# The last convolution layer of a four-layer image network: 1x1 products first, depthwise taps second, in place of convolutions folded into stacked planes

## The reference, cut to what matters

```python
def _edffn(x, w_in, w_dw, fft_w, w_out):          # x: group-normed, 48 channels
    h = jnp.einsum('bchw,oc->bohw', x, w_in)       # 1x1 products: 48 -> 192 channels
    h = conv(h, w_dw, 'SAME', feature_group_count=192)   # depthwise 3x3 taps
    x1, x2 = jnp.split(h, 2, axis=1)               # 96 and 96 channels
    h = gelu(x1, approximate=False) * x2
    y = jnp.einsum('bchw,oc->bohw', h, w_out)      # 96 -> 48 channels
    # 8x8 patches: f = rfft2(patch) * fft_w; y = irfft2(f)
    return y
x = x + _edffn(_gn(x), ...)
```

## Time and profile before

| | us |
|---|---|
| median of 3 runs | 21097.66 |
| the profiled execution | 21103.45 |
| its span, first to last instruction | 21101.9 |
| TensorE busy | 19033.5 (90%) |
| VectorE busy | 13401.1 (64%) |
| GpSimd busy | 10333.9 (49%) |
| ScalarE busy | 7503.4 (36%) |
| mean granted TensorE clock | 0.955 |

### The profile page before, as it was taken

How to read it: one execution, slowest core, us unless ns; L and a number is a source line. 1 busy time by engine, 2 the same in 40 slices (tenths; PEclk the granted TensorE clock), 3 DMA queues, 4 the chain that set the end, 5 groups by cost and what they waited for, 6 DMA issues and landing times. The chain is left out here.

```text
span 21101.9 us, 501412 instructions
## 1 busy us (share of the span) xinstructions
PE 19033.5 (90%) x172464; PEld 11794.6 (56%) x172464; DVE 13401.1 (64%) x22319; ACT 7503.4 (36%) x22720; POOL 10333.9 (49%) x8692
## 2 busy tenths in 40 slices
PE   6998998989989989899899898999998989898999
PEld 4665455456655554566555445665555456565666
DVE  4444445656667776666677766666777667777744
ACT  3554232145542221455422214663222122222222
POOL 0000000067767740677677406886774078787810
PEclk9999999999999999999999999999999999999999
DMA  3231112655533336455333364553434666666633
GB/s 92 68 70 45 35 36 84 140 112 113 113 99 111 110 119 145 109 112 113 99 110 111 112 151 111 121 121 100 111 110 126 134 146 150 149 149 146 147 88 78
DMA packets 932423, 2318.18 MB, mean 110 GB/s; under 512 B 276340, under 2 KB 528504, under 8 KB 844124
## 3 DMA queue, kind: packets, MB, share of 16 engines
q1 hardware_dynamic: 500560, 1364.68, 27.8%
q0 software_dynamic: 430080, 928.96, 16.7%
HBM read 1915.53 MB, written 385.13 MB: 109 GB/s over the span
## 5 line engine op out<-in xcount | busy, mean ns | idle before, releaser
L1840 POOL DMA_INDIRECT e_got<-table,e_idx x6144 | 7479.2, 1217 | 2580.1 <-issue 1603.5
L1856 POOL DMA_INDIRECT e_got<-table,e_idx x2048 | 2553.1, 1247 | 691.6 <-issue 501.7
L1010 PE MATMUL b_p_conv<-b_z,b_diag 32*32 32x512 f32 x76032 | 2807.1, 599 | 3.3 <-issue 3.3
L530 PE MATMUL a_p_qk<-a_wst,a_stack 125*128 125x192 f32 x12288 | 2466.8, 337 | 230.9 <-ACT a_qh L661 214.0
L530 PEld LDWEIGHTS a_p_qk<-a_wst,a_stack 125*128 125x128 f32 x12288 | 2025.8, 191 | 670.5 <-issue 367.5
L1112 ACT ACTIVATE b_z<-b_p_z 128x256 f32<-128x256 f32 x2112 | 846.5, 401 | 4026.9 <-PE b_p_z L974 3608.2
L1894 DVE TENSOR_TENSOR e_got<-e_got,e_wt 128x1536 f32<-128x1536 f32 x1024 | 1778.6, 1752 | 684.9 <-DMA e_got<-table,e_idx 682.3
L1199 DVE TENSOR_TENSOR b_ym<-b_p_in,b_mask 128x512 f32<-128x512 f32 x1056 | 729.4, 691 | 1807.8 <-PE b_p_in L966 1807.6
L974 PEld LDWEIGHTS b_p_z<-const,b_ym 128*128 128x128 f32 x8448 | 1165.3, 198 | 1215.5 <-issue 713.3
L974 PE MATMUL b_p_z<-const,b_ym 128*128 128x128 f32 x8448 | 1541.1, 307 | 100.1 <-ACT b_z L1112 93.9
L2140 PE MATMUL d_p_v<-d_xs,d_ws 125*128 125x512 f32 x4608 | 1388.2, 449 | 64.0 <-issue 60.4
(11 more groups left out here) (291 smaller groups left out, 35444.6 us busy)
## 6 DMA issues: line engine op xcount, KB each, us to landing
e_got<-table,e_idx POOLq DMA_INDIRECT x8192
b_x<-planes SPq DMA_DIRECT2D x264, 395.1 KB
a_stack<-in_xp SPq DMA_DIRECT2D x256, 387.0 KB
c_stack<-planes SPq DMA_DIRECT2D x256, 387.0 KB
d_stack<-planes SPq DMA_DIRECT2D x512, 193.5 KB
table<-i_acc SPq DMA_DIRECT2D x256, 384.0 KB, 2.3
b_xr<-planes SPq DMA_DIRECT2D x264, 197.5 KB
planes<-b_out SPq DMA_DIRECT2D x264, 197.5 KB
```

Source lines behind the costliest of these rows:

```text
L530: m = pe.matmul(dst_, st[:, row, dx + 128 * t:dx + 128 * t + 128], wst[:, dx, 0:2 * C2], start=(dx == 0), stop=False)
L1010: mm = pe.matmul(p_conv[q // 2 * 2 + r % 2][BLK * c:BLK * (c + 1), :], diag[g][BLK * r:BLK * (r + 1), k, :], zs[BLK * r:BLK * (r + 1), g, ...
L1840: pool.indirect_dma_start(out=self.got[q][:, t, c * REC:(c + 1) * REC], out_offset=None, in_=self.flat, in_offset=bass.IndirectOffsetOnAxi ...
L1856: pool.indirect_dma_start(out=self.got[q][:, t, c * REC:(c + 1) * REC], out_offset=None, in_=self.flat, in_offset=bass.IndirectOffsetOnAxi ...
```

## The change

`layer3` is written anew; the gathers, the spectrum, the residual and all other layers stay. `load_half` is gone.

- Loads: instead of 22 DMAs into stacked planes, a strip has 2: the same 49 planes of 9 rows go to partitions 0 to 48 and 64 to 112 of `x`.
- 1x1 products, in full fp32, into two PSUM banks `p_z`: for each of 4 quarters, two products of two rows each. `hidden_big` makes 128 channels by 64x128 tiles (2 in a pair), `hidden_small` the other 64 channels by 64x32 tiles (8), at two row offsets, so that a block of 32 channels lies twice on the partitions.
- ACT copies each quarter (128x1024) from `p_z` to `z` in SBUF, and once a strip two rows that the next strip needs.
- Depthwise taps as products with diagonal matrices: `taps_big`, 9 rounds (one for each tap) of sixteen 32x32 tiles into all four banks `p_v`; `taps_small`, 6 rounds of eight 64x32 tiles into two of them.
- ACT takes 3 gelus of 128x512 (before 6 of 64x512), DVE makes 3 products of 128x512 (before 6 of 64x512). `upper` and `lower` are gone from this layer.
- PSUM: `p_a` serves both the product with `w_out` and the spectrum (before `p_a` and `p_b`), one bank `p_c` the way back and the turned boxes (before two). A strip's taps need all four banks, so the next strip's taps wait for all products of this one.
- Beats: 64 in 3 strips as before, now counted over 15 rounds of taps a strip. DVE's order of box parts and products is new.
- Weights: 6 DMAs at the start of an image instead of 16, among them the image's first three rows.

```diff
+                def hidden_big(i, xs, row):
+                    r = 64 * i
+                    return pe.matmul(p_z[:, i, :], w[r:r + CP, 0:128], xs[r:r + CP, row:row + QROWS, 1:1 + W], start=True, stop=True)
+                def hidden_small(bank, r, xs, row):
+                    for t in range(4):
+                        y = row + t % 2
+                        mm = pe.matmul(p_z[BLK * t:BLK * t + BLK, bank, :], w[r:r + CP, 128 + BLK * t:128 + BLK * t + BLK],
+                                       xs[r:r + CP, y:y + QROWS, 1:1 + W], start=True, stop=True)
+                def hidden(n, xs, j):
+                    g, h = divmod(j, 2)
+                    pe.wait_ge(z_copied, n * 4 + j)
+                    for i in range(2):
+                        row = 2 * QROWS * h + QROWS * i
+                        mm = hidden_small(i, 64 * i, xs, row) if g else hidden_big(i, xs, row)
+                    mm.then_inc(h_ready, 1)
...
+                    def taps_big(lo, hi):
+                        if lo == 0:
+                            pe.wait_ge(z_copied, (n + 1) * 4)
+                            pe.wait_ge(zrow_ready, n + 1)
+                            pe.wait_ge(g_ready, n * 3)
+                        for i in range(lo, hi):
+                            dy, dx = divmod(i, 3)
+                            for row in range(4):
+                                for c in range(4):
+                                    q = PERM[row][c]
+                                    mm = pe.matmul(p_v[q // 2 * 2 + row % 2][BLK * c:BLK * (c + 1), :], diag[0][BLK * row:BLK * (row + 1), i, :],
+                                                   z[k][BLK * row:BLK * (row + 1), 0, dy:dy + SROWS, dx + QX * q:dx + QX * (q + 1)],
+                                                   start=(i == 0), stop=(i == 8))
+                    def taps_small(lo, hi):
+                        if lo == 0:
+                            pe.wait_ge(g_ready, n * 3 + 1)
+                        for i in range(lo, hi):
+                            y, dx = divmod(i, 3)
+                            for row in range(2):
+                                for c in range(4):
+                                    mm = pe.matmul(p_v[row][BLK * c:BLK * (c + 1), :], diag[1][64 * row:64 * (row + 1), i, :],
+                                                   z[k][64 * row:64 * (row + 1), 1, y:y + SROWS, dx + QX * c:dx + QX * (c + 1)],
+                                                   start=(i == 0), stop=(i == 5))
...
+                    # TensorE's order in a strip
+                    ahead(0); turn_box(0); taps_big(0, 3); w_out(0); turn_box(1); ahead(1); taps_big(3, 6)
+                    spectrum(0); ahead(2); taps_big(6, 9); inverse(0, 0); w_out(1); ahead(3)
+                    taps_small(0, 2); inverse(0, 1); spectrum(1); taps_small(2, 4); inverse(1, 0)
+                    taps_small(4, 6); inverse(1, 1)
...
+                    # VectorE's order in a strip
+                    box residual; box_part(0); [box residual]; box_part(1); scale(0); box_part(2)
+                    product(0); product(1); residual(0, 0); box_part(3); residual(0, 1)
+                    scale(1); residual(1, 0); product(2); residual(1, 1)
```

More of the change, by code:

```diff
@@ L2136, in conv_big @@
[L2136 to L2143, removed]
-                        mm = pe.matmul(out, we[i][0:NREST, lo:lo + 128], part(xe[j][0:NREST, :, :], side), start=False, stop=(i, j) == HALVES[-1])
-                    mm.then_inc(conv_ready, 1)
@@ L2147, in conv_small @@
-                def conv_small(bank, i, h, beats):
-                    tiles = [(bank[SMALL * k:SMALL * k + SMALL, :], HID * (k // 2) + BIG, k % 2) for k in range(4)]
-                    rows = slice(HROWS * h, HROWS * (h + 1))
-                    for dx in range(3):
-                        for out, lo, side in tiles:
-                            mm = pe.matmul(out, wst[:, dx, lo:lo + SMALL], part(stack[i][:, rows, dx:dx + W], side), start=(dx == 0), stop=False)
-                        if dx in beats:
-                            boxes.beat(mm)
-                    for k, (out, lo, side) in enumerate(tiles):
-                        mm = pe.matmul(out, wrs[0:NREST, lo:lo + SMALL], part(rest[i][0:NREST, rows, 0:W], side), start=False, stop=True)
-                        if k == 0 and 3 in beats:
-                            boxes.beat(mm)
-                    mm.then_inc(conv_ready, 1)
+                    pe.matmul(p_v[0][:, 0:NW], fold[:], win[:], start=True, stop=True).then_inc(folded, 1)
@@ L2162, in step @@
+                    pe.wait_ge(w_ready, 2 * (b + 1))
+                    hidden_big(0, x0, 0)
+                    hidden_small(1, 0, x0, 0).then_inc(folded, 1)
+                    pe.wait_ge(loaded0, (b * U + 1) * 32)
+                    pe.wait_ge(zrow_ready, n0 + 1)
+                    for j in range(4):
+                        hidden(n0, x[0], j)
                 def step(v, r, n, front, back, more):
                     m = n - 1
+                    k = r % 2
+                    units = turned(v, r) if boxes and back else []
@@ new lines, in ahead, with turn_box @@
+                    def ahead(j):
+                        if more:
+                            if j == 0:
+                                pe.wait_ge(loaded[1 - k], (b * U + v * 3 + (r + 1) // 2 + 1) * 32)
+                            hidden(n + 1, x[1 - k], j)
+                    def turn_box(j):
+                        if j < len(units):
+                            if j == 0:
+                                pe.wait_ge(res_ready, m * 4)
+                            else:
+                                boxes.bank_free(pe, *units[0])
+                            boxes.turn(pe, *units[j], p_c)
@@ L2203, in step @@
[L2203 to L2221 removed]
+                    ahead(0)
@@ new lines, in step @@
+                    turn_box(0)
+                    if front:
+                        taps_big(0, 3)
+                    if back:
+                        w_out(0)
+                    turn_box(1)
+                    ahead(1)
+                    if front:
+                        taps_big(3, 6)
+                    if back:
+                        spectrum(0)
+                    ahead(2)
+                    if front:
+                        taps_big(6, 9)
+                    if back:
+                        inverse(0, 0)
+                        w_out(1)
@@ L2338, in step @@
[L2338 to L2359 removed]
+                        dve.tensor_tensor(rows, p_c[0:CP, :].rearrange("p (t y x) -> p t y x", y=SROWS, x=16), rows, ALU.add).then_inc(res_ready, 1)
@@ new lines, in step @@
+                    if units:
+                        boxes.residual(dve, *units[0], p_c)
+                    box_part(0)
+                    if len(units) > 1:
+                        boxes.residual(dve, *units[1], p_c)
+                    box_part(1)
+                    if back:
+                        scale(0)
+                    box_part(2)
+                    if front:
+                        product(0, gb[k][0], p_v[1], ga[0])
+                        product(1, gb[k][1], p_v[3], ga[1])
```

376 lines of the change are left out of this document (176 added, 200 removed).

## The result

The changed kernel takes 23048.58 us (median of 4 runs, 23041.22 to 23052.24) against 21094.35 us before (4 runs, 21084.56 to 21103.62). The ratio is 1.0925, 95% interval 1.0909 to 1.0941: 1954 us slower, where I forecast 147 faster. It is also above the high end of my range.

The account below looks back on a forecast made before the run. GpSimd was taken to bound the joint stage, TensorE the lone one. A joint gain of 171 us and a lone loss of 25 took 21103.45 to 20957, put at 20950 us; range 20830 to 21140.

Parts of the forecast that it names:

- The step that failed: SyncE's queue: 2 loads replace 22, 0.9 MB instead of 1.6, a strip ahead, nothing later; put at nothing.
- Rival 4: VectorE's order: late box parts hold products and banks, TensorE 34.2 us a strip, total 21235 us; chance 0.12.
- GpSimd's side: Joint stage: without `lower`, gathers get shorter, 33.1 to 31.2 us a strip, stage 3271 to 3089 us.
- the forecast's sum for GpSimd alone: Joint stage if only GpSimd bounds it: 3089 us, a gain of 182.
- Rival 3: Joint stage: gathers stay as long beside `weigh` and `halve`, stage 3271 us, total 21125 us; chance 0.08.
- TensorE's side: Layer 3's convolution: 20.0 us a strip out, 20.7 in, so the strip goes from 28.4 to 29.1 us.
- rival 1: TensorE's taps: tiles cheaper, 0.91 us a round, strip 25.7 us, total 20835 us; chance 0.17.
- Rival 2: TensorE: each change of tile shape costs time, strip 31.1 us, total 21110 us, no change; chance 0.13.
- The waits inside a strip: New PSUM waits mostly hidden; in the joint stage `turn_box` waits for the last residual, 0.3 us a strip.
- the starts of images: Fewer weight DMAs against four quarters and copies before the first taps: 0 in the joint stage, +3 us in the lone.

Follow-up runs that it names:

- e1: Changed kernel with the load of a strip's planes put ahead of SyncE's wait for the residual, more than a strip earlier: 21024.71 us, ratio 0.9973 to before.
- e4: Kernel before, with `lower` in the last layer's strips cut to 8 columns, so lower halves of operands are left out: 20884.70 us, ratio 0.9905.
- e8: e1 with GpSimd allowed 60 beats ahead instead of 36 and the turned box moved behind the first chunks of taps: 21012.59 us, ratio 0.9960.
- e7: Kernel before, with only the second half of a strip's refill moved behind the store and its wait for the residual: 22131.89 us against 21099.17.
- e9: Changed kernel, load still late, each DMA of 49 partitions split into 48 and 1, four DMAs in all: 22943.76 us, one run.

## Why the prediction was wrong

**The step that failed** is the one on DMA: 2 loads of 49x9 rows "a strip ahead. SP's queue gets shorter, so nothing behind it is later". The sum had it at nothing. I counted how many DMAs the queue holds, and their bytes, and not when each is issued against when its data is first read. The load is two strips ahead by its index, but its issue stands behind a wait for the end of a strip, and its first reader moved to the front of one. That the queue is shorter was true, and the wrong question: what counts is the wait ahead of the load and the start of its reader. e1 puts the price of this at 2024 us: 1867 of idle time at `hidden`, and clock. TensorE was busy 3175.56 + 1011.95 us in the changed kernel and 2980.36 + 950.91 in e1, with the same instructions: 256 us. Together 2123 us, about 100 more than the 2024; in e1 GpSimd's pace and other waits stand in their place. I had no rival for it. Rival 4 was also a late input, but of VectorE's order, and ends far below.

The other steps, with the load in its place (e1):

- **GpSimd's side was right.** Mean gather 1.169 us, put 1.16; 21.33 x 600 / 408 = 31.4 us a strip, put 31.2. e4, `lower` gone alone, gave 199 us; the forecast's sum for GpSimd alone was 182. Rival 3 falls. One reading was slightly off: two of the 388 gathers, of 1.18 and 1.14 us at 17312.92 and 17513.32, stand beside `finish` (L1906, L1908) and not beside `weigh`, `halve` or `lower`.
- **TensorE's side was right.** Strip 29.05 us against 29.1. A round of sixteen tiles took 3.35 / 3 = 1.12 us, within layer 1's 1.07 to 1.21. The strip of 27 that rival 1 worked out, as an estimate, from the 4 ns for a further tile in the Trainium skill ("TensorE: Matmul & The Clock Gate", Measured speedup vs the span model) did not come. Rival 2's price for a change of shape isn't seen: it put the strip at 31.1.
- **The waits inside a strip were right in sum.** `turn_box` waits for the last residual up to 1.2 us at a time, but 5.2 us in the 19 strips of the steady stretch, 0.27 each; put 0.3.
- **What was mis-sized** are the starts of images. By the first instruction of image 3, at 20155.1 before and 20039.2 in e1, the joint stage ends 116 us sooner (put 171) and the lone one 981.6 against 946.8, so 35 longer (put 25). Its first taps come 20068.65 - 20039.21 = 29.4 us after that point, before 17.3: 12 where I put 3. In order of time:

```profile
20053.67 2.08 PE L2114 MATMUL d_p_z<-d_x,d_w 49*128 49x512 f32 x4 [1.25 <-issue]
20056.95 2.08 PE L2114 MATMUL d_p_z<-d_x,d_w 49*128 49x512 f32 x4 [1.21 <-ACT d_z L2273]
...
20068.65 4.08 PE L2165 MATMUL d_p_v<-d_z,d_diag 32*32 32x512 f32 x64
```

  Five quarters in a row, with ScalarE's copy between each two, run at a granted clock of 0.50: 3.2 us a quarter, where I had 2.3. In the joint stage I put 0 for this, against three such starts. Against GpSimd's own sum of 182, 66 us are missing there: the gathers took 1.474 us each with their gap, where I had 1.463, which is 23; and they stood still for 89 us beyond their gaps (17 to 18.5 at a border) against 67 before, which is 22. The other 21 no row divides; I had put 11, for two engines so close to each other.

The mechanism that I forecast exists, then, and is worth 59 us as the change was made (e1) and 87 with e8's edits; one wait outweighed it more than twenty times. As the expectation of e1 shows, I took that wait for the whole cause at once, and e7, which makes it in the old design, shows that the new layer isn't needed for it.

The fastest run here has no new layer at all: it is e4, the old layer without `lower`, and e4 leaves a part of the product out. Whether the old layer can do without it at the wanted precision was not tried.

## What to carry to other kernels

For every load that a change touches, write down two moments from the trace: when its queue can issue it (behind which wait, and what ends that), and when its first reader starts; the slack is the difference, and a load "two strips ahead" by index can have none. A change that moves a reader earlier in its turn uses up slack even if the load itself is smaller. The Trainium skill says it as a rule ("DMA: Bandwidth & Descriptors", Rules for kernel authors: "Issue the DMA early, do compute, wait on its semaphore late"), and the runs agree: with 11.4 us from issue to first reader TensorE waited 13.5 us a strip, with 37.9 us it did not wait. When two engines are within a few per cent of each other, as here, do not count on more from a relief of one than their distance.

## What the hardware showed that I had not expected

- A load of 49 partitions had 7 packets in flight for most of its time in e1 (4.6 of 6.1 us); the split into 48 and 1 (e9) had up to 16 and more: as an estimate, 7 of the 16 DMA engines.
- 889 KB in two loads of 49 partitions took 11.4 us from issue to use; with 1 of 9 rows in the second (444.4 x 10/9 = 494 KB) it was 9.98 us, and in four DMAs (e9, issue at 22344.26, use at 22353.76) 9.5.
- A wait of 13 us costs TensorE clock as well: 2.08 us instead of 1.13 for the first product, 4.50 instead of 3.42 for the first chunk of taps.
- TensorE's stream has a gap of 2 to 3 us once in every six strips that no semaphore explains, with a lower clock behind it (0.66 in the 5 us of taps below): in e1 at 20296.93, 20476.54 and 20655.87, of which the last

```profile
20655.87 1.13 PE L2114 MATMUL d_p_z<-d_x,d_w 49*128 49x512 f32 x4 [2.12 <-issue]
20656.93 5.01 PE L2165 MATMUL d_p_v<-d_z,d_diag 32*32 32x512 f32 x96
```

  and in the kernel before, at 20395.99, 20569.87 and 20743.94 (2.11, 1.87 and 2.03 us). Both kernels' program for this layer is a loop with six strips in its body (`PER` = 6), so the gap comes with its turn; what in the turn costs the time isn't shown. It is in both kernels, so it explains no difference.
